# State-space stage of a six-stage decoder: the chain for the time steps in two halves, one beside the MoE tiles and one in the scan

## The reference

```python
x = x + L0_ffn(layernorm(x), ...)                   # stage C: 8 experts, top 2, and a shared expert
x = x + L1_attn(layernorm(x), ...)                  # stage D:
    xBCzA = in_proj(x)                              # 1536 conv channels, 512 of z, 64 of A_log
    xBC   = silu(causal_conv(xBC, 4 taps) + bias)   # -> x: 64 heads x 8, B and C: 8 groups x 64
    dt    = softplus(A_log)                         # per token and head
    x_in  = x / dt
    y_ssm = ssd_chunk_scan(x_in * dt, -dt, B, C, chunk=128)
        A_cum  = cumsum(-dt) within a chunk
        Y_diag = (C B^T * exp(segsum(-dt))) X
        Y_off  = C (state of the chunk before) * exp(A_cum)
    y     = y_ssm + D * x_in
    out   = out_proj(y * silu(z + z_bias))
```

## Time and profile before

| | us |
|---|---|
| median of 3 runs | 995.91 (994.95 to 996.75) |
| the profiled execution | 990.7 |
| its span in the trace | 988.9 |
| PE busy | 810.5 (82%) |
| VectorE / ScalarE / GpSimd busy | 577.0 / 383.7 / 216.6 |

### The profile page before, as it was taken

How to read it: one execution, slowest core, us unless ns; L and a number is a source line. 1 busy time by engine, 2 the same in 40 slices (tenths; PEclk the granted TensorE clock), 3 DMA queues, 4 the chain that set the end, 5 groups by cost and what they waited for, 6 DMA issues and landing times.

```text
span 988.9 us, 14763 instructions
## 1 busy us (share of the span) xinstructions
PE 810.5 (82%) x5680; PEld 523.6 (53%) x5680; DVE 577.0 (58%) x1188; ACT 383.7 (39%) x653; POOL 216.6 (22%) x210
## 2 busy tenths in 40 slices
PE   1577777599799799656999999998667786899998
PEld 0334443258677588533445444444445454677776
DVE  5666642544545457525878788568566653545443
ACT  1124334101444355233566465354124344444442
POOL 3200000223433322141101111011411201442432
PEclk9889979799999899866989899699778788899999
DMA  9000001001121211000000000000000001222331
GB/s 311 29 2 1 3 1 49 1 0 32 49 81 53 71 54 33 9 0 5 5 3 6 4 5 6 3 5 4 1 2 2 1 1 50 81 80 64 84 96 40
DMA packets 17831, 32.77 MB, mean 33 GB/s; under 512 B 5819, under 2 KB 9787, under 8 KB 17494
## 3 DMA queue, kind: packets, MB, share of 16 engines
q1 hardware_dynamic: 17762, 31.83, 10.4%
HBM read 29.85 MB, written 1.05 MB: 31 GB/s over the span
## 4 chain that ended last, share of the span: by engine, by line
PE 60%; DVE 20%; issue 9%; ACT 4%; POOL 4%; DMA 1%; SPq 1%; DVEq 0%; ACTq 0%; POOLq 0%
PE bank L1374 13%; PE bank L1398 8%; PE bank L1136 4%; PE bank L1484 3%; PE bank L1321 3%; PE bank L1482 3%; PE bank L1411 3%; PE bank L1418 2%; DVE s_xn L1555 2%; PE bank L1336 2%; DVE s_arena L1627 2%; PE bank L1265 2%; POOL s_rstd L739 1%; PE bank L1208 1%; PE bank L1384 1%
## 5 line engine op out<-in xcount | busy, mean ns | idle before, releaser
L791 POOL TENSOR_TENSOR s_wl<-s_wmoe,s_wh 128x768 fp32r<-128x768 f32 x54 | 99.2, 1839 | 175.0 <-ACT s_wh L961 175.0
L910 ACT ACTIVATE s_arena<-bank 128x512 f32<-128x512 f32 x96 | 56.6, 597 | 106.2 <-PE bank L1241 55.2
L1746 DVE TENSOR_TENSOR s_act<-bank,s_sg_moe 128x512 f32<-128x512 f32 x54 | 37.3, 691 | 82.4 <-PE bank L1374 75.8
L1627 DVE TENSOR_REDUCE s_arena<-bank 128x2 f32<-128x512 f32 (+1 forms) x96 | 64.6, 686 | 35.6 <-PE bank L1212 18.9
L1374 PE MATMUL bank<-s_xh,s_wh 128*128 128x512 f32 x216 | 73.1, 421 | 8.2 <-POOL s_wl L791 8.2
L973 ACT CAST s_ah<-s_act 128x512 fp32r<-128x512 f32 x54 | 33.6, 621 | 101.7 <-DVE s_act L1751 79.2
L1374 PE MATMUL bank<-s_xl,s_wh 128*128 128x512 f32 x216 | 69.3, 403 | 0.0
L1398 PE MATMUL bank<-s_wh,s_ah 128*128 128x256 f32 x216 | 66.5, 308 | 2.8 <-DVE s_al L1757 2.8
L1374 PE MATMUL bank<-s_xh,s_wl 128*128 128x512 f32 x216 | 68.4, 399 | 0.0
L1781 DVE SCALAR_TENSOR_TENSOR s_arena<-s_arena,s_convw 128x256 f32<-128x256 f32 x144 | 63.7, 483 | 0.6
L1398 PE MATMUL bank<-s_wl,s_ah 128*128 128x256 f32 x216 | 61.6, 285 | 0.0
(11 more groups left out here) (232 smaller groups left out, 1745.6 us busy)
## 6 DMA issues: line engine op xcount, KB each, us to landing
s_wmoe<-in_wF SPq DMA_DIRECT2D x28, 384.0 KB, 3.1
s_wmoe<-in_wC SPq DMA_DIRECT2D x26, 384.0 KB, 3.0
s_win<-in_win SPq DMA_DIRECT2D x1, 2112.0 KB, 10.4
s_x<-in_x SPq DMA_DIRECT2D x4, 256.0 KB, 3.5
s_early<-in_ctxT SPq DMA_DIRECT2D x1, 1024.0 KB, 9.5
s_ctxn<-in_ctx SPq DMA_DIRECT2D x1, 1024.0 KB, 12.3
s_arena<-s_arena SPq DMA_DIRECT2D x64, 6.0 KB
out_x<-s_x SPq DMA_DIRECT2D x4, 256.0 KB, 2.8
```

The costliest lines, as they stand in the source:

```text
L791: g.tensor_tensor(wl[:, w % NS_, :], wmoe[:, w % NW, :], wh[:, w % NS_, :], ALU.subtract).then_inc(wl_ready, 1)
L910: a.activation(PT[:, p % NPT, :], AR[n % 3][:, :], ACT.Exp).then_inc(a_read, 1)
L1627: v.tensor_reduce(nM[:, q, h0:h0 + heads], V[n % 2][:, :].rearrange("p (h k) -> p h k", h=heads), AX.X, ALU.max, negate=True).then_inc(v_r ...
L1746: v.tensor_tensor(act_[:, w % 2, :], G[2 * (n % 2) + 1][:, :], sg_moe[:, n % 2, :], ALU.mult).then_inc(g_read, 1)
```

## The change

It cuts the chain for the time steps into two halves of 4 units (256 columns instead of 512), each with steps of its own. The first half (units 0 to 3, batches 0 and 1) stands beside tiles 4 to 10 of the second half of the MoE stage; the second (units 4 to 7) stands in slots 21 to 44 of the scan, which are in units 1 and 2. The transposes `lt` of batches 2 and 3 move to slots 2 and 3 of the scan. The border keeps `at`, `xt`, `xt1`, z. Pair 8 becomes the first pair in the scan, so that each later pair stands one place earlier in the row of three, and the last, pair 23, is in unit 5. The two memsets of the spread buffers move into the first two `xtp`. The tiles of the chain get their own space in `early`, since the arena's `M`, `yo` and `yf` are in use by then.

```diff
-FIRST_PAIRS = 9
+FIRST_PAIRS = 8
...
+LATER_TURNS = (2, 3)
+SECOND_STEPS = ((21, "dt_in"), (22, "dtc"), (23, "dt_p1"), (24, "dt_a1"), (25, "dt_p2"), (26, "dt_a2"), (27, "dt_p3"), (28, "dt_a3"),
+                (29, "dt_sum"), (33, "acum"), (34, "acumc"), (37, "last"), (38, "lastc"), (39, "dec_in"), (40, "dec_exp"),
+                (41, "ap_hi"), (42, "ap_mid"), (43, "ap_lo"), (44, "ddt"))
+BESIDE_C_STEPS = ((4, "dt_in"), (4, "dtc"), (4, "dt_p1"), (5, "dt_a1"), (5, "dt_p2"), (5, "dt_a2"), (6, "dt_p3"), (6, "dt_a3"),
+                  (6, "dt_sum"), (7, "acum"), (7, "acumc"), (8, "last"), (8, "lastc"), (8, "dec_in"), (9, "dec_exp"),
+                  (9, "ap_hi"), (9, "ap_mid"), (10, "ap_lo"), (10, "ddt"))
...
                     if nxt == "D" and hf == 1:
+                        steps.extend((kind, nxt, 0) for at_j, kind in BESIDE_C_STEPS if at_j == j)
                         if 0 < j - 4 <= beside_c:
                             taps(j - 5)
...
-            while late:
-                turn(*late.pop(0))
-            steps.append(("dt_in", s, 0))
-            chain = ["dt", "acum", "at", "atc", "ddt"]
-            for m in range(beside_c, FIRST_PAIRS):
-                din(m)
...
-            steps.extend((kind, s, 0) for kind in ("zth", "zsm", "xt", "xtc", "xtp", "xt1", "xt1c"))
+            steps.extend((kind, s, 0) for kind in ("at", "atc", "xt", "xtc", "xtp", "xt1", "xt1c", "dz", "dz2", "zt", "zth", "zsm"))
...
+            for slot, (stage, b) in zip(LATER_TURNS, late):
+                put(slot, "lt", b)
+            late.clear()
+            for slot, kind in SECOND_STEPS:
+                put(slot, kind, 1)
...
                 elif kind == "dt_in":
                     bk = t_bank("dt_in", s, i)
-                    pe.wait_ge(t_read, at["T"]["lt", s, B - 1] + 1)
-                    for u in range(NU):
+                    pe.wait_ge(mix_in, 96)
+                    pe.wait_ge(t_read, at["T"]["lt", s, 2 * i + 1] + 1)
+                    for n in range(NU // 2):
+                        u = NU // 2 * i + n
...
+                elif kind in ("acum", "last"):
+                    pe.wait_ge(dt_ready, 2 * i + 1)
+                    bk = t_bank(kind, s, i)
+                    mm(bk[:, 0:HV], tri[:, int(kind == "last"), :], t_max, start=True, stop=True).then_inc(t_full, 1)
```

More of the change, by code:

```diff
@@ L319, in number @@
             fill("V", kind, s, i)
-        if kind == "acum":
-            for k in range(2):
-                fill("T", kind, s, k)
+        if kind in ("acum", "last"):
+            fill("T", kind, s, i)
         if kind == "qkv_mm" and s == "A":
@@ L833, in _ @@
                     pool.wait_ge(r_read, at["R"]["xt", s, i] + 1)
-                    pool.wait_ge(dt_ready, 2)
+                    pool.wait_ge(dt_ready, 2 * half_of(i) + 2)
+                    if i < 2:
+                        link(g.memset(xsp[i], 0.0))
                     if i >= 2:
@@ L1010, in _ @@
                                  ).then_inc(tanh_ready, 1)
-                elif kind == "dt_in":
+                elif kind == "dtc":
                     act.wait_ge(t_full, at["T"]["dt_in", s, i] + 1)
-                    a.copy(t_a, T[:, :]).then_inc(t_read, 1)
+                    act.wait_ge(halved, 1)
+                    if i:
+                        act.wait_ge(ap_ready, i)
+                    a.copy(t_a, T[:, 0:HV]).then_inc(t_read, 1)
                 elif kind == "zth":
@@ L1811, in _ @@
                 elif kind == "ddt":
[L1812 to L1819 removed]
+                    dve.wait_ge(dt_ready, 2 * i + 1)
@@ new lines, in _ @@
+                    half = ddt[:, HV * i:HV * (i + 1)]
+                    link(v.reciprocal(half, t_max))
+                    v.tensor_tensor(half.rearrange("p (u h) -> p u h", h=NV), half.rearrange("p (u h) -> p u h", h=NV),
+                                    dskip[:, :].unsqueeze(1).to_broadcast([P, NU // 2, NV]), ALU.mult).then_inc(dt_ready, 1)
+                elif kind == "dec_in":
+                    dve.wait_ge(t_read, at["T"]["last", s, i] + 1)
+                    cum, last, d3 = (a.rearrange("p (b c h) -> p b c h", c=NT, h=NV) for a in (t_a, t_u, dec[:, HV * i:HV * (i + 1)]))
@@ L1834, in _ @@
-                    ins.then_inc(ap_ready, 1)
+                    api = ap_[:, NU // 2 * i:NU // 2 * (i + 1)]
+                    if kind == "ap_hi":
+                        for h in range(2):
+                            ins = v.tensor_copy(api[:, :, h, :, 0, :], cum[:, :, h])
+                        link(ins)
+                    elif kind == "ap_mid":
+                        for h in range(2):
+                            ins = v.tensor_tensor(rest[:, :, h], cum[:, :, h], api[:, :, h, :, 0, :], ALU.subtract)
+                        link(ins)
+                    else:
+                        for h in range(2):
+                            ins = v.tensor_copy(api[:, :, h, :, 1, :], rest[:, :, h])
+                        link(ins)
+                        for h in range(2):
+                            ins = v.tensor_tensor(api[:, :, h, :, 2, :], rest[:, :, h], api[:, :, h, :, 1, :], ALU.subtract)
+                        ins.then_inc(ap_ready, 1)
```

99 lines of the change are left out of this document (37 added, 62 removed).

## The result

The changed kernel takes 968.49 us (median of 4 runs, 960.61 to 970.65), the kernel before 995.43 in the same comparison: ratio 0.9715, 95% interval 0.9679 to 0.9751. The forecast was 954 and its range 944 to 968: the change is faster, but 14.5 us less so than I said, with the median 0.5 us above the upper end of the range. The profiled execution took 966.35 us, its span is 964.6 (before 990.7 and 988.9). In the runs further down, one execution of e4 (979.4 us, the one that has the trace) and one of e8 (988.1) fell in a slower state and are left out of the medians and ranges.

What follows compares the result with a forecast made beforehand. TensorE sets the pace except at the 45.7 us serial border and in low-clock stalls; -39.0 + 6.3 + 1.5 + 7.0 - 10.5 - 7.0 = -41.7 gives span 947.2, with 5.2 and the span-to-time difference carried over 954 us, range 944 to 968.

Steps and rivals of the forecast that it cites:

- sign of being wrong: Clock of 0.50 inside units 1 to 5, tiles over 7 us besides 4, 7 and 8, or border over 10 us.
- Border: Between MoE stage and scan: the dt chain's first half is already done, so 6.7 us in place of 45.7, -39.0.
- Beside the tiles: MoE tiles 4 to 10: first half's matmuls, copy waits and late ScalarE +6.3, possible clock drop +1.5; bounds 3.4 and 15.
- rival 2: MoE tiles 6 to 8: chain late by a whole tile, deeper stall, 964 us (about 961 by table-load drain); chance 12%.
- In the scan: Scan: transposes and a wait +1.7, second half's matmuls +2.9, table reloads +0.5, one pair more in unit 5 +1.9; together +7.0.
- units 1 and 5: Scan: shifted pairs remove unit 1's wait and low clock, -5.0; unit 5's state-matmul wait goes and clock stays up, -7.0.
- Unit 3: Scan: with pair 18 second, the `ev` wait and the low clock behind it go, -5.5 (bounds 0 and -6.2).
- rival 1: Scan: border gain comes, but new stalls in units 1, 2 or 5 keep the low clock; 970 us, chance 17%.
- Rivals 2, 3 and 4: 3: tiles 4 to 11 at low clock, all eight 1005 us, 2%. 4: something else ends late at the border, 960, 9%.

Runs made afterwards that it cites:

- e4: Changed kernel with the first half's four ScalarE functions replaced by Silu, so its seven table loads beside the tiles are gone (computes something else): 953.4 us.
- e8: Changed kernel with the edits of e1, e5 (norm for stage E in slot 6 of the odd unit) and e6 together: 973.2 us.
- e6: Changed kernel with the steps of the chain's first half spread wider over the MoE tiles, same instructions and as many table loads: 975.1 us.
- e2: Kernel before with only the shift of the pairs: pair 8 leaves the border and becomes the scan's first pair; 992.75 us, ratio 0.998.
- r0: The changed kernel measured again, unedited, as reference for the other runs: 966.22 us, ratio to before 0.9699.
- e1: Changed kernel with the second half's `ddt` (reciprocal and product D/dt on VectorE) moved from slot 44 to slot 57: 957.06 us.
- e3: Changed kernel with the chain's first half taken from beside the MoE tiles and put in one piece at the head of the border: 971.4 us.
- e9: Kernel of e6 with `th` of a unit's second pair in slot 13, not 12, behind the third pair's `ev`: 961.13 us.
- e12: Changed kernel with the first half spread as in e6, `th` in slot 13 and second-half `ddt` in slot 57, norm left alone: 956.62 us.
- e10: Kernel of e8 with `th` of the second pair in slot 13 and the norm for stage E in slot 10 of the odd unit: 959.42 us.
- e11: Kernel of e10 without the spread, the first half standing where the changed kernel has it: 961.76 us.

## Why the prediction was right, and where it was off

The direction, the border and most of the terms came out as forecast; two thirds of the gain were reached (27 us of 42). The sign of being wrong that did occur is a clock of 0.50 inside units 1 to 5, in unit 3. Term by term, in spans, predicted and found:

- **Border** -39.0, found -38.1. Right, and by its own steps: `at` to score matmul 6.6 predicted and 6.67 found.
- **Beside the tiles** +6.3 and +1.5 for the clock, found +8.7, with no fall of the clock. TensorE's own work is 1.9 + 1.3 us (1.8 and 1.1 estimated). Tiles 4, 7 and 8 gained 2.5, 3.1 and 1.2 us (2.2, 3.1 and 1.0 predicted), tile 7's being two waits, 0.86 ahead of `acum` and 1.30 behind it, and `acum` itself. What I missed is VectorE: `ddt` in tile 10 takes 2.2 us, as I had from no row, and the 6 us that I counted between `al` and its use did not hide it: the wait for the last `al` is 1.5 us longer. In e6, with the reciprocal in tile 8, it is back at 1.43. The 1.5 booked for the clock and this miss about cancel, which is luck. The drain of rival 2 does not show: in this trace an activation starts 0.01 us after its table load ends (load at 362.86 for 1.28 us, Exp at 364.15), and e4 finds 2.5 us for seven loads.
- **In the scan** +7.0 for the second half, the transposes and the pair, **units 1 and 5** -5.0 and -7.0. Unit 0 +1.4 (1.7 predicted), units 1 and 2 together -1.3 (-1.6), unit 5 with its pair -6.7 (-5.1). Right in kind. The shift of the pairs alone gives -4.7, -5.2 and -6.7 in e2, so the terms for units 1 and 3 hold. In unit 5 both parts were mis-sized: it is 2.8 us longer than unit 6 now (1.9 for the pair), and all of the 9.5 us of its excess went (-7.0).
- **Unit 3** -5.5, found +3.4 in this trace (-2.7 in r0's). This is the step that failed, by 8.9 us here and 2.8 there. The prediction said "walking through the new order I find no wait over 1 us"; there is one of 0.97 and one of 1.33, since I walked through TensorE and ScalarE there and not through VectorE, whose new 2.2 us of `ddt` stand just ahead of a norm. e1 takes them away and finds -5.3.
- **Unit 7** 0, found +7.0 (42.92 against 35.95). No step of mine looked at it, for the change moves nothing in it. The wait is the same in both; the clock behind it was kept for 20 us in the traces of before and e3 and lost within 3 us in changed, r0, e1, e2, e4, e6, e9 and e12.
- **Ahead of the change** +2.7, a drift that no edit made; behind unit 7 -1.4.

Of the miss of 17.4 us in the span (947.2 against 964.6), 8.9 are unit 3, 7.0 are unit 7 and 2.7 drift; the rest, -1.2, is small change. The mechanism that I gave 17% in rival 1 (new stalls keep the low level) is the right one for unit 3; it had named units 1, 2 and 5. Its time of 970 is near the measured one by luck: it gives up 15.5 of the 17.5 us booked for units 1, 3 and 5, and units 1 and 5 did give theirs. Rivals 2, 3 and 4 did not occur.

Open: what decides whether the clock falls behind a wait of 0.5 to 1.3 us. Taking the wait away kept it up each time (unit 3 in e1, e10, e11 and e12; unit 1 in e9), but behind the same wait with the same work around it the clock fell in some traces and not in others, and in e2's unit 0 it stayed low for over 30 us with no wait at all. Not tried: the norm of stage E in small pieces between the slots, which might take the wait of unit 7 away without a new one.
